# The first layer of a four-stage block: one stream of 64 pairs of heads in place of five loops of heads

## The reference, cut to what matters

```python
def _L0_attn_ref(hidden_states, Wq, Wkv, Wo):      # 32 heads of 16, one key/value head
    q = (hidden_states @ Wq).reshape(b, s, 32, 16)
    kv = hidden_states @ Wkv
    k, v = (kv[..., :16], kv[..., 16:])
    scores = jnp.einsum('bqhd,bkd->bhqk', q, k) * 16 ** -0.5
    bias = slopes[:, None, None] * (pos[None, None, :] - pos[None, :, None])
    scores = jnp.where(causal[None, None], scores + bias[None], -jnp.inf)
    attn = jax.nn.softmax(scores, axis=-1)
    out = jnp.einsum('bhqk,bkd->bqhd', attn, v).reshape(b, s, h)
    return out @ Wo
def _L0_ffn_ref(x, q_scales, q_vals, bias):
    return jnp.einsum('bsi,oi->bso', x, _dequantize(q_scales, q_vals)) + bias
...
x = x + _layernorm(_L0_attn_ref(_layernorm(x), ...))
x = x + _layernorm(_L0_ffn_ref(_layernorm(x), ...))
x = x + _layernorm(_L1_attn_ref(_layernorm(x), ...))
x = x + _layernorm(_L1_ffn_ref(_layernorm(x), ...))
```

## Time and profile before

| | |
|---|---|
| median of 3 runs | 2521.51 us (2521.39 to 2526.22) |
| the profiled execution | 2520.12 us, its span 2518.3 us |
| mean granted clock of PE | 0.944 |
| busy, whole span | PE 85%, DVE 74%, ACT 61%, POOL 27% |
| first layer | from about 60 us to 824 us of the span |

### The profile page before, as it was taken

The page is one execution under the profiler, slowest core; times in us unless marked ns, Lnnn a source line. Parts: engine busy times, 40 slices in busy tenths (PEclk is TensorE's granted clock), DMA queues, the critical chain, the costliest instruction groups (busy, mean ns, idle before and its releaser), DMA issues. The chain is left out here.

```text
span 2518.3 us, 49756 instructions
## 1 busy us (share of the span) xinstructions
PE 2146.9 (85%) x18352; PEld 1310.3 (52%) x18352; DVE 1864.5 (74%) x4645; ACT 1531.5 (61%) x3606; POOL 688.4 (27%) x563
## 2 busy tenths in 40 slices
PE   6688777778774589999999999999999999758997
PEld 2465555555552255555555555655555556423443
DVE  3688897897995477777777777777777777575554
ACT  2587776777771376667667676667666767341221
POOL 0312212111110243343433343334333333112221
PEclk9899899889997799999999999999999999978999
DMA  5101001000000343444334434443344333320000
GB/s 203 33 2 35 1 7 47 2 18 18 2 18 17 115 81 63 89 87 91 80 66 89 81 71 82 80 91 78 64 89 84 66 68 65 72 87 17 34 17 34
DMA packets 380593, 147.59 MB, mean 59 GB/s; under 512 B 354928, under 2 KB 359664, under 8 KB 378304
## 3 DMA queue, kind: packets, MB, share of 16 engines
q1 hardware_dynamic: 380352, 144.41, 25.5%
HBM read 48.95 MB, written 11.53 MB: 24 GB/s over the span
## 5 line engine op out<-in xcount | busy, mean ns | idle before, releaser
L1157 ACT ACTIVATE xp<-xp,nm 128x128 f32<-128x128 f32 (+3 forms) x512 | 281.3, 550 | 354.5 <-DVE nm L1236 354.5
L1017 POOL TENSOR_TENSOR q_in_sbuf<-q_in_sbuf,sinq 128x512 f32<-128x512 f32 x128 | 231.2, 1806 | 688.2 <-ACT q_in_sbuf L1145 581.3
L1207 DVE SCALAR_TENSOR_TENSOR probs_lo<-xp,rl,probs_hi 128x128 f16<-128x128 f32 (+3 forms) x512 | 263.5, 576 | 109.4 <-ACT probs_hi L1122 109.4
L575 ACT ACTIVATE xp<-xp,nm 128x512 f32<-128x512 f32 (+3 forms) x512 | 249.8, 569 | 50.9 <-DVE nm L680 49.1
L680 DVE CUSTOM_DVE_ANT_0 xp<-bank,tab,cs 128x512 f32<-128x512 f32 (+3 forms) x512 | 250.2, 545 | 4.3 <-PE bank L459 2.0
L1236 DVE CUSTOM_DVE_ANT_0 xp<-bank,mask,cs 128x128 f32<-128x128 f32 (+3 forms) x512 | 250.3, 545 | 0.0
L1122 ACT ACTIVATE probs_hi<-xp,rl 128x128 f16<-128x128 f32 (+3 forms) x512 | 244.0, 549 | 0.7 <-DVE rl L1256 0.7
L472 PE MATMUL bank<-ident,xp 128*128 128x128 f32 x1280 | 182.7, 291 | 62.6 <-ACT xp L575 45.6
L1041 PE MATMUL bank<-xT_hi,wq_hi 128*128 128x512 f16 x512 | 195.2, 381 | 43.2 <-DVE yacc L1251 37.4
L708 DVE TENSOR_TENSOR pT_lo<-bank,pT_hi 128x384 f16<-128x384 f32 (+1 forms) x384 | 207.1, 593 | 32.5 <-ACT pT_hi L543 32.4
L1041 PE MATMUL bank<-p1T_hi,v_hi 128*128 128x128 f16 x1280 | 223.0, 220 | 2.9 <-DMA p1T_lo<-probs_lo 2.9
(11 more groups left out here) (235 smaller groups left out, 5535.9 us busy)
## 6 DMA issues: line engine op xcount, KB each, us to landing
raw_q<-in_wq SPq DMA_DIRECT2D x8, 1024.0 KB, 5.3
raw_o<-in_wo SPq DMA_DIRECT2D x8, 1024.0 KB, 5.6
x_front<-in_x SPq DMA_DIRECT2D x4, 1024.0 KB, 5.8
xb<-in_x SPq DMA_DIRECT2D x4, 1024.0 KB, 7.1
x_scratch<-xb SPq DMA_DIRECT2D x4, 1024.0 KB, 4.4
x_before<-x_scratch SPq DMA_DIRECT2D x4, 1024.0 KB, 5.6
wup<-in_wup SPq DMA_DIRECT2D x3, 1024.0 KB, 11.9
fused_scratch<-fused SPq DMA_DIRECT2D x12, 256.0 KB, 2.4
```

What stands on the lines that cost most here:

```text
L575: act.activation(x, x, ACT.Exp, scale=-1.0, bias=nm[:, h % 4, t:t + 1]).then_inc(s_ex, 1)
L1017: pool.tensor_tensor(qs[:, i % 2, :], qs[:, i % 2, :], rope["sink" if u[0] == "k" else "sinq"][:, :], ALU.mult).then_inc(s_rot, 1)
L1157: ins = act.activation(x, x, ACT.Exp, scale=-1.0, bias=nm[:, m % 3, t:t + 1], accum_out=ls[:, m % 3, t:t + 1])
L1207: ins = dve.scalar_tensor_tensor(pr[1][:, m % 2, c], xp[:, m % 3, c], rl[:, m % 3, t:t + 1], pr[0][:, m % 2, c], ALU.mult, ALU.subtract)
```

## The change

`layer0` is written anew. Run and loop are gone: the layer is one block with one stream of NP = 64 pairs of heads (16 per batch), counted by a step n from -20 to 98. In step n each engine does its part of several pairs: the maxima of pair n, the exponentials of pair n-6, the product with the values of pair n-8, the division of pair n-9. The rest of a batch's work stands at fixed steps (`FRONT`, `BACK`), counted from the batch's first pair.

- **Scores twice.** The first pass gives the scores with queries on the rows; DVE takes only the row maximum, straight from the bank (5 instructions per pair, L874 to L879). The maxima of four pairs are joined, transposed, split, and carried by four DMAs into rows of the query stack. The second pass gives the exponents with keys on the rows: bias and negative maximum are rows of the stacks, the mask is a product of its own (`far` with `tri` or `tri_T`). So the exponential (ACT, L714, 5 of 512 per pair) gives the weights in the orientation in which the values need them, and no transposes are left.
- **Stacks.** The 128 rows hold hi and lo of two heads' queries, slopes and maxima. 24 DMAs per four pairs put the queries there (L412), in place of the selecting products.
- **Weights split in parts.** The weights lie in SBUF (two pairs deep). POOL casts all five parts to hi (L487: 1,024, 1,024, 512), and makes the lo part of the last (L489); DVE makes the lo parts of the first four (L888, two of 1,024). The product with the values has 40 matmuls per pair (34 and 17 columns).
- **Banks.** Three for the first pass, three for the exponents, two for everything else.
- **Norms.** POOL makes the root and the shift (three operations), ACT the normalising (L707), POOL the adding of rows; POOL divides the heads pair by pair (L476, L478), four small operations.

Its core:

```diff
-        def run(b, attend, back, front):
...
-        run(-1, False, False, True)
-        run(0, True, False, True)
-        with nc.Fori(1, B - 1) as b:
-            run(b, True, True, True)
-        run(B - 1, True, True, False)
-        run(B, False, True, False)
+        NP = B * PAIRS
+        X_LAG, V_LAG, N_LAG = 6, 8, 9
+        STEPS = range(-20, NP + N_LAG + 26)
+        FRONT = {"load": -16, "norm": -11, "n1": (-8, -7), "V": -6, "K": -5}
+        BACK = {"load": 27, "o": (14, 17, 21, 26), "y": (28, 28, 29, 29), "add1": 30, "n2": (32, 34),
+                "f": (36, 36, 38, 38), "add2": 39, "n3": (46, 47)}
+        groups = {"s": banks[0:3], "x": banks[3:6], "rest": banks[6:8]}
...
+                def stack_queries(g):
+                    sp.wait_ge(s_qd, g + 1)
...
+                    for h in range(8):
+                        for lo, r in ((0, 16), (1, 32), (0, 48)):
+                            to = 64 * (h % 2) + r
+                            sp.dma_start(qs[to:to + E0, g % GP, h // 2, :],
+                                         qq[lo][h * E0:(h + 1) * E0, g % 2, :]).then_inc(s_qs[g % 2], 16)
...
+                def norm_heads(p):
...
+                    for e in range(2):
...
+                        pool.tensor_tensor(od[:, :, :], o[:, :, 0:E0], o[:, :, EV:EV + E0], ALU.add).then_inc(s_os, 1)
+                        pool.wait_ge(s_os, 2 * p + e + 1)
+                        pool.tensor_tensor(on[:, :, c:c + E0], od[:, :, :],
+                                           ro[:, p % 3, e, :].unsqueeze(2).to_broadcast([P, TT, E0]),
+                                           ALU.mult).then_inc(s_on, 1)
+                def weights_hi(p):
+                    if p >= 2:
+                        pool.wait_ge(s_pf, p - 1)
+                    for i, (c0, c1) in enumerate(((0, 2), (2, 4), (4, 5))):
+                        pool.wait_ge(*emptied[("x", p, c1 - 1)])
+                        pool.tensor_copy(ph[0][:, p % 2, c0:c1, :], px[:, p % 2, c0:c1, :]).then_inc(s_wh, 1)
+                    pool.wait_ge(s_wh, 3 * p + 3)
+                    pool.tensor_tensor(ph[1][:, p % 2, 4, :], px[:, p % 2, 4, :], ph[0][:, p % 2, 4, :],
+                                       ALU.subtract).then_inc(s_wc, 1)
...
+                def scores(p, i):
...
+                    for e, t, c in PARTS[i]:
+                        w = P * (t + 1)
+                        pe.matmul(out[:, c:c + w], qs[:, g % GP, pp, t * P:(t + 1) * P], kz[:, g // GP % 2, e, 0:w],
+                                  start=True, stop=False)
+                        ins = pe.matmul(out[:, c + w - P:c + w], far[:, :], tri[:, :], start=False, stop=True)
+                def exponents(p, i):
...
+                    for e, j, c in XPARTS[i]:
+                        pe.matmul(out[:, c:c + S - j * P], ks[:, g // GP % 2, e, j * P:(j + 1) * P],
+                                  qs[:, g % GP, pp, j * P:S], start=True, stop=False)
+                        ins = pe.matmul(out[:, c:c + P], far[:, :], trit[:, :], start=False, stop=True)
...
+                def exponential(p, i):
+                    if p >= 2 and i in (0, 2, 4):
+                        act.wait_ge(*((s_wl, 2 * (p - 2) + 1), (s_wl, 2 * (p - 2) + 2), (s_wc, p - 1))[i // 2])
+                    act.wait_ge(*filled[("x", p, i)])
+                    act.activation(px[:, p % 2, i, :], bank_of(("x", p, i))[:, :], ACT.Exp,
+                                   scale=unit[:, 0:1]).then_inc(s_ed, 1)
...
+                def weights_lo(p, i):
+                    c = slice(2 * i, 2 * i + 2)
+                    dve.wait_ge(s_wh, 3 * p + i + 1)
+                    if p >= 2:
+                        dve.wait_ge(s_pf, p - 1)
+                    dve.tensor_tensor(ph[1][:, p % 2, c, :], px[:, p % 2, c, :], ph[0][:, p % 2, c, :],
+                                      ALU.subtract).then_inc(s_wl, 1)
...
-            for n, shape, dt in (("rel", [P, S], F32), ("sel", [P, 8, P], F16), ("pairmask", [P, 2], F32),
-                                 ("bias", [P, D], F32)):
+            for n, shape, dt in (("rel", [P, S], F32), ("bias", [P, D], F32)):
```

More of the change, by code:

```diff
@@ new lines, in layer0 @@
+        fillings = {"s": [], "x": [], "rest": []}
+        for n in STEPS:
+            if 0 <= n < NP:
+                fillings["s"] += [("s", n, i) for i in range(5)]
+            if 0 <= n - X_LAG < NP:
+                fillings["x"] += [("x", n - X_LAG, i) for i in range(5)]
+            if 0 <= n - V_LAG < NP:
+                fillings["rest"].append(("pv", n - V_LAG))
+            if n % GP == 0 and 0 <= n // GP - 1 < NG:
+                fillings["rest"].append(("m", n // GP - 1))
+            fillings["rest"] += others(n)
@@ new lines, in layer0, with bank_of @@
+        for u in fillings["s"] + fillings["x"] + fillings["rest"]:
+            full, empty = signals[u[0]]
+            counted[full] = counted.get(full, 0) + 1
+            filled[u], emptied[u] = (full, counted[full]), (empty, counted[full])
+        def bank_of(u):
+            k, i = place[u]
+            return groups[k][i % len(groups[k])]
+        norms, adds = [], []
+        for n in STEPS:
+            for kind, when in (("n1", FRONT["norm"]), ("a1", BACK["add1"]), ("n2", BACK["add1"] + 1),
+                               ("a2", BACK["add2"]), ("n3", BACK["add2"] + 1)):
+                if at(n, when) is not None:
+                    norms.append((kind, at(n, when)))
+                    if kind in ("a1", "a2"):
+                        adds.append((kind, at(n, when)))
```

1017 lines of the change are left out of this document (577 added, 440 removed).

## The result

The kernel after the change takes 2,537.2 us, median of five runs (2,533.4 to 2,542.5), against 2,521.9 for the kernel before on the same chip: ratio 1.0058, 95% interval 1.0042 to 1.0074. It is 0.6% slower. The forecast was 2,471 us, 2% faster; the time lies inside the range given, and on the side that had a chance of 0.28.

A forecast was written before the change was run, and what follows sets the result against it. GpSimd was taken as the bound: 64 pairs at 7.85 us (502) plus batch work made 580 us from the first cast at 124.5; with the tail the layer ends at 773.5, 50 us gained: 2,471 us, range 2,380 to 2,600.

The forecast's parts named there:

- first maximum: Head: VectorE's first row maximum at about 104 us, 15.5 later, after tiny operations, ScalarE's fills and 24 query DMAs.
- the stream, 64 pairs: Attending part from the first cast at 124.5 us: GpSimd's 64 pairs plus what batches add, 580 us.
- tail: Layer's end after the stream: 12 us of last product, small operations and adding, then 57 us, ending at 773.5.
- The pair on GpSimd: Casts, subtraction and small operations of one pair: 5.6 us, with the conflict 7.85 us; 64 pairs 502 us.
- the conflict: VectorE's two 1,024-wide subtractions with SBUF inputs and GpSimd's casts exclude one another: GpSimd loses 2.26 us per pair.
- what a batch adds to it: GpSimd's added load in the attending part: roots 21 us, row additions 26, hold during ScalarE's normalising and exponentials 31.
- Rival E: Four fixed-order queues with one pair of slack stall each other by 0.8 us per pair: 2,521 us; chance 0.10.
- not the bound at the full clock: PE in the attending part: 4.05 us per pair plus projections and transposes per batch, 381 us in total.
- rival D: PE's granted clock stays at the lower level; at 1.2 GHz throughout, 7.1 us per pair, 2,549 us; chance 0.06.
- the signs named: 1,024-column casts 1.1 us, subtractions over 1.2, some 9 us per pair, GpSimd over 85% busy; wrong if it waits throughout.
- B: Rival: casts are cheap and VectorE is the bound, 2,413 us with lock waits, 2,336 without; chance 0.27.
- C: Rival: a GpSimd cast costs as much as a two-input operation, 1.27 us per 512, giving 2,682 us; chance 0.17.

The follow-up runs named there:

- norms_aside: Changed kernel with ScalarE's normalising moved between the next step's fourth and fifth exponentials, GpSimd's row addition behind the next pair's casts and heads: 2476.4 us.
- root_first: norms_aside with ScalarE's normalising back at the end of its own step, GpSimd's addition still later: 2557.0 us.
- aside_onepart: norms_aside with every first-layer projection made of hi x hi alone, 4 products in place of 12, the rest left out: 2429.0 us.
- aside_small: norms_aside with GpSimd's four small operations per pair (64 elements each) joined into two of 128: 2467.3 us.
- best version: Changed kernel with norms_aside, ScalarE casting weight parts 3 and 4, key stacks built later, head_dma and head_iota together: 2450.2 us, ratio to before 0.9713.
- head_iota: Changed kernel with GpSimd writing the slopes before the row of positions, and ScalarE's query-stack fills taking another input: 2533.4 us.
- head_dma: Changed kernel with 12 of the 24 query DMAs of each of the first two groups issued from ScalarE: 2533.7 us.

## Why the prediction was wrong

The error of 70 us in the layer's end, by the prediction's own steps:

| step | forecast | measured |
|---|---|---|
| first maximum | 104 | 115.7 |
| from there to the first cast | 20.5 | 31.6 |
| the stream, 64 pairs | 580 | 609.3 |
| tail | 69 | 86.6 |

Head and tail make 40 of the 70 us, the stream 29, which is what is left of two larger errors of opposite sign.

**The pair on GpSimd was right in kind and too dear.** 7.85 us were forecast, 7.05 measured; prices without the conflict 5.1 (forecast 5.6), the conflict 1.55 (2.26), since I let every VectorE subtraction shut GpSimd out for its whole length; that some of them fall where GpSimd waits anyway is my reading and was not tested. 64 x 7.05 = 451 us, not 502. By luck this error hid 51 of the next one's 80 us.

**The step that failed is "what a batch adds to it": 78 us, measured 609 - 451 = 158.** I priced a norm as work of GpSimd (root and adding) and a hold of 3.9 us in which it has nothing to cast. I wrote down that ScalarE normalises after GpSimd's root and then makes the next exponentials, and even what stands behind it, but took the hold as ScalarE's own work alone. Not counted was that ScalarE stands still before that, some 7 us at each norm: 4.0 until VectorE has the variance, 0.8 until GpSimd is at the root, 2.4 for its three operations. norms_aside gives 52 us of the stream back; against root_first, from which it differs in ScalarE's place alone, it is 69. Rival E was this mechanism, with a price of 51 us for the stream, but I spread it over all pairs and gave it 0.10; the trace has it at 12 places. PE's projections, which I costed off the path ("not the bound at the full clock"), carry another 30 us, measured with the norms aside (aside_onepart); the step with two products and the keys takes 13.6 us there in place of 16.4. PE's granted clock was 0.90 in that step and 0.59 to 0.80 in those with a norm (second and third batch), so a piece of rival D may be in it, which no run shows; the mean over the batches was 0.83 to 0.90 and not the lower level.

**Head.** VectorE's chain of tiny operations was priced right (0.2 us each), but one of them waits for GpSimd's slopes, and the statistics come at 75.4 instead of 67.4. The 24 issues take 0.63 us each and not 0.50. Then ScalarE again waits for a root, that of batch 1's front, with the first exponentials behind it; with the norms aside the way from the first maximum to the first cast is 3.5 us shorter:

```profile
69.55 0.56 POOL L449 IOTA weights<- 128x512 f32 x1 [42.17 <-issue]
...
71.62 0.24 DVE L780 TENSOR_SCALAR weights<-weights,runit 128x32 f32<-128x32 f32 x1 [5.41 <-POOL weights L454]
75.36 2.47 DVE L804 BATCH_NORM_STATS2 st<-x_front 128x6 f32<-128x512 f32 x4
...
98.58 0.64 SPq L412 DMA_DIRECT2D q_stack<-q_hi  x1
99.27 0.58 SPq L412 DMA_DIRECT2D q_stack<-q_lo  x1
...
115.74 1.29 DVE L874 TENSOR_REDUCE mx<-bank 128x1 f32<-128x512 f32 x2 [10.96 <-PE bank L544]
...
143.23 2.93 ACT L707 ACTIVATE x_front<-x_front,nb,rs 128x512 f32<-128x512 f32 x4 [10.10 <-POOL nb L465]
146.06 2.38 ACT L714 ACTIVATE weights<-bank,unit 128x512 f32<-128x512 f32 x4
```

**Tail.** The heads' last transposed tiles stand on ScalarE behind the last norm of batch 2, so that they come 19.6 us after the last `weights_lo` instead of 12; from there the layer needs 66.9 us, where the kernel before needed 61.5 and I took 57:

```profile
764.84 4.93 POOL L499 TENSOR_TENSOR xb<-xb,yb 128x512 f32<-128x512 f32 x4 [0.93 <-ACT yb L707]
...
772.93 2.92 ACT L707 ACTIVATE yb<-xb,nb,rs 128x512 f32<-128x512 f32 x4 [6.06 <-POOL nb L465]
775.76 0.57 ACT L666 ACTIVATE heads_T_hi<-bank 128x512 f16<-128x512 f32 x1
...
776.36 0.69 DVE L818 TENSOR_TENSOR heads_T_lo<-bank,heads_T_hi 128x512 f16<-128x512 f32 x1 [5.18 <-ACT heads_T_hi L666]
...
842.62 0.69 DVE L818 TENSOR_TENSOR xT_lo<-bank,xT_hi 128x512 f16<-128x512 f32 x1 [0.16 <-ACT xT_hi L666]
```

The overlap of statistics and adding by rows, which I credited, is there, but four rows are normalised in 2.9 us on ScalarE and added in 4.9 on GpSimd. No run was made for the tail: these causes are read from the trace alone. Two runs shortened it on the way, norms_aside to 80.5 us and aside_onepart to 68.9.

**The rivals and signs.** B (VectorE the bound) and C (dear casts) are out: the cast took 1.08 us, and the step keeps its length where VectorE is half idle. Of the signs named, the cast's price, the long subtractions (1.46 us) and 9 us per pair (9.5) came; GpSimd was busy for 76% of the stream, not over 85%, and it waited 124.5 us for ScalarE's weights, which was the sign for "wrong".

Still open: the stream of norms_aside exceeds 451 us by 106. By work, GpSimd has 12 x 1.6 us of roots and 5 x 4.9 us of additions in it, 44 us, about what I had forecast for these; the experiments took out 30 (products) and 7 (keys). How the remaining 25 are made up was not tried.

## What to carry to other kernels

When engines run through fixed queues with one item of slack, price each side job by how long the first engine in its chain stands still, with the queue of the engine that releases it read out item by item, and not by its work. A small operation that an engine has to wait for is taken up where this engine has other work in front of it: with all else alike, moving the normalisings from the end of ScalarE's step to a place behind four of the next five exponentials was worth 74 us (root_first to norms_aside). Look also at where an edit really puts an operation: the last place of a step and the first of the next are one. A busy share well under full on all engines after a rewrite is the sign to look for this before any load is moved.

## What the runs showed of the hardware

- The conflict between GpSimd and a VectorE instruction with two SBUF inputs is paid per instruction: casts of 8 or 16 columns took 0.19 to 1.27 us, operations of 64 elements 0.29 to 1.31, casts of 1,024 columns up to 2.08. Fewer and longer GpSimd instructions lose less: joining four into two gave 14 us in aside_small, though nothing that can be told on top of the best version.
- GpSimd's first `iota` starts late at both places that were tried: at 69.6 us when it is first in the layer, and after the memsets. In head_iota the memsets ahead of it run at 59.9 us and it follows 8.6 us later, with nothing in the profile that it waits for:

```profile
59.97 0.31 POOL L454 MEMSET mx<- 128x256 f32 x1
68.87 0.56 POOL L455 IOTA weights<- 128x512 f32 x1 [8.59 <-issue]
```

- A DMA of 16 partitions from SBUF to SBUF takes its queue 0.63 us to issue on SyncE (24 from 98.6 to 113.8 us) and as much on ScalarE (12 in 7.4 us, head_dma), where the engine does nothing else meanwhile.
